# Two products of a fused model rewritten as sums of rounded parts, with buffers shared and three stages moved

## Chip, cores and metric

One core of a Trainium2 chip runs the whole kernel in one launch. The metric is device time in microseconds (us), lower is better; of several runs the median is compared.

## What is computed

Sixteen samples pass one after another through a chain of layers. Each sample is 384 rows of 256 numbers: 256 rows of image edges and 128 rows of embedded text.

```python
h = concat(edges(x), (U * s @ Vt)[x_txt])                 # 16 x 384 x 256
h = h + attention(layernorm(h))                           # 16 heads of 16, window of 128 rows
h = h + top_rows(layernorm(h))                            # 288 of 384 rows: gelu(row @ w_block)
h = h + state_space(layernorm(h))                         # circulant recurrence, by its DFT
xf = layernorm(h)
shared = gelu(xf @ sw1.T + sb1) @ sw2.T + sb2             # 256 -> 1024 -> 256, every row
logits = xf @ router_w.T + router_b                       # 8 experts, the best 2 of each row
h = h + shared + sum(weight_e * expert_e(xf))             # experts: 256 -> 1024 -> 256
```

The change touches `xf @ sw1.T` (the shared network's first product) and `xf @ router_w.T` (the router's).

## The kernel before

The five engines' programs are written out by hand, each in its own function, with semaphores between them; an engine runs its instructions strictly in that order. The samples form a software pipeline: `sequence(b)` runs, on each engine, the attention of sample b, together with the *head* of sample b+1 (edges, text, normalisation, queries, keys, values), the *chain* of sample b-1 (row selection, state space, router, first shared product) and the *late* part of sample b-2 (second shared product, slot rows for the experts). Sequences 0 and 1 and the last two are written out, since parts are missing there (sequence 0 has no chain); those between are a loop. After sequence 17 the experts' stage gathers rows by expert and runs in chunks to the end; the change touches its weights' loads only.

A sequence has 33 slots, s = 0 to 32. Slots 0 to 23 each start one *unit* of the attention (two heads for 128 query rows): PE makes scores, DVE their maximum (`mx`), ACT the exponentials (`prob`), PE turns them (two slots later), ACT evicts (`pT`), PE multiplies with the values. The rest is placed in numbered slots, and in its slot it stands in an engine's queue before or behind that slot's unit. These matter here:

- Slot 1, DVE: `own` (L1215) and the rank trials (L1221, L1224) of sample b-1, behind the eviction of `srow` on ACT (L844); the trials write their products into `rot` and `cum` and go on in slots 2 and 3. They stand before unit 1's maximum (L1150).
- Slots 2 to 8, PE: the six pieces of the second shared product (`down`, L1716), the text's turn in slot 3 and its product in slot 5 (L1564), which waits for DVE's `usT` (L1088, slot 4).
- Slot 21, DVE: `xn` of sample b+1 (L1063), then the third statistics of the chain (`chain_rows(b, 2)`, L1038). POOL then works out the deviations, DVE normalises `xc` in slot 26 (L1063), and POOL adds the shared network's bias (`shared_residual`, L666).
- Slots 24 to 27: ACT evicts xT (L789), PE multiplies the queries of b+1 (slot 26), turns xc and multiplies the keys (slot 27); ACT evicts the queries (q_hi, q_full) and then the turned xc as `xcT`; DVE splits the keys into k_hi and k_lo (L1118, L1122), then makes q_lo (L1129).
- Slots 28 to 32, PE: the logits (L1773), the values (L1600), the output product and the eight blocks f of the first shared product (`up`, L1703; six of them behind slot 32).

An f32 product appears on PE as two instructions for each pair of a weight tile and a moving tile. Where attention needs products of rounded parts already (scores, edges, experts), a float32 is held as `hi` (rounded to fp32r) and `lo` (the rest), and hi*hi + hi*lo + lo*hi is added up.

SP's queue (`stack(b + 1)`) copies the parts of the queries and keys into the stacked operands `qs` and `ks`, 36 transfers a sample in four pairs of head groups: 8 of q_hi, then for each pair 4 of k_hi, 1 of q_lo, 2 of k_lo. It starts when the queries are evicted (`q_ready`), behind the store of xc (`xn_rows`). Each pair has a semaphore `stacked[pair]`, and PE waits for it where the pair is first used:

```python
                    m, r = g % KB, g // KB
                    if i == 0 and m == 0:
                        pe.wait_ge(stacked[r].sem, stacked[r].at(b, stacked[r].per))
```

that is in slots 0, 2, 4 and 6. For sample 0 the keys are stacked by `stack_first_keys`, and DVE builds the powers of the recurrence's eigenvalues in slots 2 to 10 of sequence 0 (`powers`, which uses `rot`).

Of the kernel before, what the change touches and what calls it, by code (L numbers as in the profile page):

```python
# [57 lines left out]
LATER = (OUT + 2,)  # L58
# [21 lines left out]
def build(nc, t):  # L80
    with ExitStack() as ctx:
# [46 lines left out]
        rank_cols = sb("rank_cols", [P, T])  # L128
# [10 lines left out]
        rw = sb("rw", [P, KB, NE])  # L139
        rb_row = sb("rb_row", [P, NE])  # L140
        sw1 = sb("sw1", [P, KB, F])
# [45 lines left out]
        k_hi = room("k_hi", [P, KB, T], F32R)  # L187
        k_lo = room("k_lo", [P, KB, T], F32R)
# [16 lines left out]
        xc = room("xc", [P, NT, D])  # L205
        xcT = room("xcT", [P, KB, T])
# [4 lines left out]
        g = room("g", [P, NT, D])  # L211
        rot = room("rot", [P, 4, T])
        cum = room("cum", [P, 2, T])
        st = room("st", [P, 2, T])
# [4 lines left out]
        hb2 = room("hb2", [P, NT, D])  # L219
        hid = room("hid", [P, FB, T])  # L220
# [3 lines left out]
        dft, idft, b_w, c_wT = (mats[:, n] for n in range(4))  # L224
        place = place[:, 4 * KB * D:]
# [7 lines left out]
        with ExitStack() as space:  # L233
# [39 lines left out]
        late_loaded = dma_signal("late_weights_loaded", 0)  # L273
        set_up = signal("constants_ready", 0)
# [150 lines left out]
            (rb_row, t["rb"].partition_broadcast(P)), (sw1, t["sw1"]), (sw2, t["sw2"]), (sb1, t["sb1"]),  # L425
# [29 lines left out]
        def _(sp):  # L455
# [82 lines left out]
            load_image(1)  # L538
            load_halo(1)
# [46 lines left out]
        def _(pool):  # L586
# [174 lines left out]
        def _(act):  # L761
# [68 lines left out]
            def turned_rows(b, n):  # L830
# [8 lines left out]
                act.activation(xcT[:], ps[:, 6:8, 0:T], ACT.Copy).then_inc(xcT_ready.sem, 1)  # L839
# [29 lines left out]
            def sequence(b, att, late, chain, head, first_weights=False):  # L869
                for s in range(SLOTS):  # L870
                    if head and s in (CONV + 2, CONV + 4):
                        magnitude(b + 1, (s - CONV) // 2 - 1)
# [41 lines left out]
            sequence(0, True, False, False, True)  # L914
# [44 lines left out]
        def _(dve):  # L959
# [20 lines left out]
            def constants():  # L980
# [9 lines left out]
                for i in range(NT):  # L990
                    dve.tensor_scalar(before[:, i], rank_cols[:], rank_own[:, i:i + 1], None, ALU.is_lt)
                    dve.tensor_scalar(after[:, i], rank_cols[:], rank_own[:, i:i + 1], None, ALU.is_ge)
# [120 lines left out]
            def keys(b):  # L1113
# [5 lines left out]
                ins.then_inc(k_ready.sem, 1)  # L1119
                dve.wait_ge(k_ready.sem, k_ready.at(b, 1))  # L1120
# [88 lines left out]
            def chain(b, s, last):  # L1209
# [9 lines left out]
                if RANK <= s < RANK + NT:  # L1219
                    i = s - RANK  # L1220
                    dve.scalar_tensor_tensor(out=trial[2 * i], in0=srow[:], scalar=own[:, i:i + 1],  # L1221
                                             in1=before[:, i], op0=ALU.is_ge, op1=ALU.mult,
                                             accum_out=count[:, 0, i:i + 1])
                    ins = dve.scalar_tensor_tensor(out=trial[2 * i + 1], in0=srow[:], scalar=own[:, i:i + 1],  # L1224
                                                   in1=after[:, i], op0=ALU.is_gt, op1=ALU.mult,
# [49 lines left out]
                if s == OUT + 2:  # L1275
                    chain_rows(b, 2, last)
# [73 lines left out]
            def sequence(b, att, late, chained, head, ahead, first=False, first_weights=False):  # L1350
                att_step.steps = 0
                for s in range(SLOTS):
                    if first and s == 1:
                        eigenvalues()
                    if first and 2 <= s < 2 + (T - 1).bit_length():
                        powers(2 ** (s - 2))
                    if first_weights and s in (TURN1, STATE + 4):
                        split_first(s == STATE + 4)
                    if chained and s not in LATER:
# [9 lines left out]
                    if chained and s in LATER:  # L1369
# [5 lines left out]
                    if head and s == TEXT + 3:  # L1375
                        text_in(b + 1)
                    if first and s == TURN1 - 1:
# [6 lines left out]
                    if head and s == UP - 1:  # L1384
                        keys(b + 1)
# [41 lines left out]
            keys(0)  # L1427
# [4 lines left out]
            dve.wait_ge(late_loaded.sem, late_loaded.at(0, NLATE))  # L1432
            sequence(1, True, False, True, True, True)
# [90 lines left out]
        def _(pe):  # L1524
# [67 lines left out]
            def values(b):  # L1592

                pe.wait_ge(ctx_ready.sem, ctx_ready.at(b, 0))
                for i in range(NT):
# [5 lines left out]
                ins.then_inc(proj_done.sem, 1)  # L1601
# [96 lines left out]
            def up(b, f):  # L1698
# [70 lines left out]
            def logits(b):  # L1769
                    pe.wait_ge(xcT_ready.sem, xcT_ready.at(b, 3))  # L1770
                    for i in range(NT):
                        for k in range(KB):
                            ins = pe.matmul(ps[:, 7, i * NE:(i + 1) * NE], xcT[:, k, i * P:(i + 1) * P], rw[:, k],  # L1773
                                            start=(k == 0), stop=(k == KB - 1))
                    ins.then_inc(logit_done.sem, 1)

            def sequence(b, att, late, chained, head, first=False, last=False):
                for s in range(SLOTS):
# [8 lines left out]
                    if head and s == UP + 2:  # L1787
                        values(b + 1)
# [32 lines left out]
                    if chained and s == TURN2 + 1:  # L1821
# [29 lines left out]
            values(0)  # L1851
# [3 lines left out]
            pe.wait_ge(late_loaded.sem, late_loaded.at(0, NLATE))  # L1855
            sequence(1, True, False, True, True, first=True)
# [129 lines left out]
```

## Time and profile before

| | us |
|---|---|
| timed runs, median of 3 | 2091.02 (2086.0 to 2092.26) |
| profiled execution | 2075.45 |
| its span, first to last instruction | 2073.7 |
| PE busy in the span | 1952.0 (94%) |
| DVE, ACT, POOL busy | 1346.1, 1069.5, 766.6 |
| mean granted TensorE clock | 0.984 of 2.4 GHz |

The profile is one execution. A row of the timeline gives the start and the length of merged instructions; a PE row's length includes the drain of its last product, so products in a row are dated by their starts. `PEld` are PE's weight loads, `SPq` is SP's queue of transfers. In brackets stands the time that an engine sat idle and what ended it. Lines (L1703) are those of the kernel above.

### The profile page before, as it was taken

The numbers are of one execution on the slowest core, as the hardware profiler recorded it, in microseconds if no ns is written. First come the engines' busy times: TensorE is split into PE (matmuls) and PEld (weight loads), VectorE is DVE, ScalarE is ACT, GpSimd is POOL, SyncE is SP. The second block draws the span as 40 slices with busy tenths as digits, with TensorE's granted clock in tenths as the row PEclk, the third lists the DMA queues.
The fourth block names the chain that finished last, engine by engine and source line by source line (L and its number), as shares of the span: only waits on it lengthen the run. The fifth ranks groups of instructions, "written<-read, shape, count | busy, mean of one in ns | idle before, by whom it ended". The sixth has DMA issues, their size and how long they took to land.

```text
span 2073.7 us, 45068 instructions
## 1 busy us (share of the span) xinstructions
PE 1952.0 (94%) x13784; PEld 1572.3 (76%) x13864; DVE 1346.1 (65%) x3781; ACT 1069.5 (52%) x2509; POOL 766.6 (37%) x1269
## 2 busy tenths in 40 slices
PE   6789999999999999999999999888999999999997
PEld 5556766667666666676666766666999999999997
DVE  5767777677676676777767767655665555656553
ACT  1545545555455555554555545541555555555553
POOL 4012333324333243232332432305354455555554
PEclk9989999999999999999999999989999999999999
DMA  5222121120211202212112021110442332323222
GB/s 172 59 47 61 33 55 44 40 68 23 56 53 29 69 28 56 59 33 54 43 41 68 23 55 38 30 54 23 130 128 44 46 89 46 89 43 87 47 46 40
DMA packets 81091, 116.56 MB, mean 56 GB/s; under 512 B 20964, under 2 KB 61508, under 8 KB 78724
## 3 DMA queue, kind: packets, MB, share of 16 engines
q1 hardware_dynamic: 54372, 84.16, 14.6%
q0 software_dynamic: 23360, 27.91, 8.2%
q10 hardware_dynamic: 3312, 3.94, 0.7%
q8 instruction: 21, 0.34, 0.1%
q14 instruction: 26, 0.21, 0.0%
HBM read 51.58 MB, written 26.71 MB: 38 GB/s over the span
## 4 chain that ended last, share of the span: by engine, by line
PE 76%; DVE 11%; issue 8%; POOL 2%; ACT 2%; ACTq 1%; DVEq 0%; DMA 0%; POOLq 0%
PE ps L1888 14%; PE ps L1703 8%; PE ps L1716 5%; PE ps L1899 4%; PE ps L1900 4%; PE ps L1901 4%; PE ps L1633 4%; PE ps L1577 4%; PE ps L1652 3%; PE ps L1549 3%; PE ps L1625 3%; PE ps L1640 2%; PE ps L1694 2%; PE ps L1754 2%; PE ps L1689 2%
## 5 line engine op out<-in xcount | busy, mean ns | idle before, releaser
L819 ACT ACTIVATE prob<-ps,mx 128x256 f32<-128x256 f32 (+1 forms) x768 | 293.9, 441 | 206.9 <-DVE mx L1150 198.5
L1150 DVE TENSOR_REDUCE mx<-ps 128x2 f32<-128x512 f32 (+1 forms) x384 | 227.2, 596 | 205.5 <-PE ps L1625 195.7
L931 ACT ACTIVATE hid_hi<-ps,b 128x256 fp32r<-128x256 f32 x408 | 203.4, 498 | 275.9 <-PE ps L1888 275.9
L811 ACT ACTIVATE pT<-ps 128x512 f32<-128x512 f32 (+1 forms) x384 | 204.2, 532 | 134.8 <-PE ps L1633 132.4
L1479 DVE TENSOR_TENSOR hid_lo<-hid_full,hid_hi 128x256 fp32r<-128x256 f32 x408 | 171.3, 426 | 143.8 <-ACT hid_full L934 143.7
L732 POOL DMA_INDIRECT result<-yb,idx_o x102 | 176.6, 1732 | 165.0 <-DVE yb L1496 143.1
L1633 PE MATMUL ps<-ident,prob 128*128 128x128 f32 x1280 | 208.0, 277 | 26.8 <-ACT prob L819 26.8
L1899 PE MATMUL ps<-w_hi,hid_hi 128*128 128x256 f32 x816 | 230.0, 282 | 0.0
L1900 PE MATMUL ps<-w_lo,hid_hi 128*128 128x256 f32 x816 | 225.5, 276 | 0.0
L1901 PE MATMUL ps<-w_hi,hid_lo 128*128 128x256 f32 x816 | 225.3, 276 | 0.0
L1633 PEld LDWEIGHTS ps<-ident,prob 128*128 128x128 f32 x1280 | 160.5, 143 | 64.6 <-ACT prob L819 30.6
L934 ACT ACTIVATE hid_full<-ps,b 128x256 f32<-128x256 f32 x408 | 203.1, 498 | 0.0
L1625 PE MATMUL ps<-ks,qs 96*128 96x512 f32 (+1 forms) x384 | 199.9, 521 | 2.3 <-ACT prob L819 2.3
L676 POOL DMA_INDIRECT slot_rows<-pay,row_i x96 | 113.3, 1180 | 220.8 <-DVE tok L1339 196.3
L1716 PE MATMUL ps<-sw,hid 128*128 128x256 f32 x768 | 185.9, 387 | 2.3 <-ACT g L846 1.0
L1703 PE MATMUL ps<-xcT,sw 128*128 128x384 f32 x512 | 174.4, 494 | 0.2 <-ACT hid L855 0.2
L1888 PE MATMUL ps<-xg_hi,w_hi 128*128 128x256 f32 x816 | 165.1, 284 | 2.5 <-DVE xg_lo L1472 1.4
L1716 PEld LDWEIGHTS ps<-sw,hid 128*128 128x128 f32 x768 | 138.8, 190 | 34.2 <-issue 11.7
L1888 PE MATMUL ps<-xg_lo,w_hi 128*128 128x256 f32 x816 | 164.4, 283 | 0.0
L1888 PE MATMUL ps<-xg_hi,w_lo 128*128 128x256 f32 x816 | 164.4, 283 | 0.0
L1900 PEld LDWEIGHTS ps<-w_lo,hid_hi 128*128 128x128 f32 x816 | 153.4, 188 | 0.0
L1899 PEld LDWEIGHTS ps<-w_hi,hid_hi 128*128 128x128 f32 x816 | 153.3, 188 | 0.0
(283 smaller groups left out, 4109.3 us busy)
## 6 DMA issues: line engine op xcount, KB each, us to landing
w_raw<-in_w SPq DMA_DIRECT2D x16, 1024.0 KB, 6.4
xin<-in_x SPq DMA_DIRECT2D x32, 384.0 KB, 3.7
ks<-k_hi SPq DMA_DIRECT2D x256, 48.0 KB, 2.1
qs<-q_hi SPq DMA_DIRECT2D x120, 96.0 KB, 2.1
ks<-k_lo SPq DMA_DIRECT2D x128, 48.0 KB, 2.1
xn_rows<-xc SPq DMA_DIRECT2D x16, 384.0 KB, 2.5
result<-h SPq DMA_DIRECT2D x16, 384.0 KB, 2.6
qs<-q_lo SPq DMA_DIRECT2D x60, 96.0 KB, 2.1
```

The costliest lines, as they stand in the source:

```text
L811: act.activation(pT[:, u % TB, :, k0:2, :], ps[:, 2 + u % 2, :].rearrange("p (h k q) -> p h k q", h=2, k=2)[:, :, k0:2, :], ACT.Copy).then ...
L819: ins = act.activation(prob[:, s % PB, hh, w], ps[:, s % 2, hh * 2 * P + w.start:(hh + 1) * 2 * P], ACT.Exp, bias=mx[:, s % 2, hh:hh + 1])
L931: act.activation(hid_hi[:, f], ps[:, f % 4, 0:CHUNK], ACT.Gelu_apprx_tanh, bias=b1[half][:, f:f + 1])
L1150: dve.tensor_reduce(mx[:, s % 2], sc, AX_X, ALU.max, negate=True).then_inc(max_done.sem, 1)
L1625: pe.matmul(dst, qs[:, r, m, i * P:(i + 1) * P], ks[:, r, :, m, keys], start=False, stop=True).then_inc(scores_done.sem, 1)
L1633: ins = pe.transpose(ps[:, 2 + u % 2, (2 * hh + k) * P:(2 * hh + k + 1) * P], prob[:, u % PB, hh, k * P:(k + 1) * P], ident[:])
L1703: ins = pe.matmul(ps[:, 6 + f % 2, 0:T], sw1[:, k, f * P:(f + 1) * P], xcT[:, k], start=(k == 0), stop=(k == KB - 1))
L1716: ins = pe.matmul(tile_out(i), hid[:, f, i * P:(i + 1) * P], sw2[:, f], start=(f == 0), stop=(f == FB - 1))
L1888: ins = pe.matmul(ps[:, f % 4, 0:CHUNK], w[half][:, k, cols], x[:, k], start=(n == 0), stop=(n == len(terms) - 1))
L1899: pe.matmul(out, hid_hi[:, f, rows], w2_hi[half][:, f], start=(f == 0), stop=False)
L1900: pe.matmul(out, hid_hi[:, f, rows], w2_lo[half][:, f], start=False, stop=False)
L1901: ins = pe.matmul(out, hid_lo[:, f, rows], w2_hi[half][:, f], start=False, stop=(f == FB - 1))
```

## The change

The shared network's first product and the router's take xf and the weights as rounded parts: `sw1_hi`, `sw1_lo`, `rw_hi`, `rw_lo` are made once, `xcT_hi` comes from ACT's eviction (in the place of `xcT`), and `xcT_lo` from a new DVE instruction, `turned_rests`, between k_hi and k_lo in slot 27. Each product becomes three fp32r products. For room, k_hi and k_lo lie in `rot`, xcT_hi in xcT, xcT_lo in `st`, the raw sw1 in the place of the start's matrices, rank_cols in hb2; the two masks `before` and `after` become shifted views of one row each. Since the rank trials and the powers write `rot`, DVE first waits for the stacked semaphores of all four pairs: in slot 1, ahead of `own`, and in slot 1 of sequence 0, ahead of the powers. sw1 is loaded by SP after the start's matrices are read, rounded by ACT in slot 12 and subtracted by DVE in slot 15 of sequence 0; the router's parts are made ahead of sequence 1. The chain's third statistics move from slot 21 to slot 22, behind that slot's unit; POOL's shared residual waits for the normalised xc of that stage; the logits move from slot 28 to 29; two of the three values products move ahead of them, to slot 28; and SP loads the experts' biases later.

```diff
-LATER = (OUT + 2,)
+LAST_STATS = OUT + 3
...
-        before = sb("before", [P, NT, T], BF16)
-        after = sb("after", [P, NT, T], BF16)
+        before_w = sb("before_w", [P, T + 2 * P], BF16)
+        after_w = sb("after_w", [P, T + 2 * P], BF16)
...
-        k_hi = room("k_hi", [P, KB, T], F32R)
-        k_lo = room("k_lo", [P, KB, T], F32R)
...
+        with ExitStack() as shared:
+            k_hi = shared.enter_context(nc.sbuf_tensor("k_hi", [P, KB, T], F32R))
+            k_lo = shared.enter_context(nc.sbuf_tensor("k_lo", [P, KB, T], F32R))
         rot = room("rot", [P, 4, T])
...
+            sp.wait_ge(mats_read.sem, mats_read.at(0, 1))
+            sp.dma_start(sw1, t["sw1"]).then_inc(sw1_loaded.sem, 16)
...
+            sequence(NB, True, True, False, False)
+            sp.wait_ge(hb2_ready.sem, hb2_ready.at(NB, 0))
             for half in range(2):
                 load_biases(half, half)
-            sequence(NB, True, True, False, False)
...
             def shared_residual(b):
 
-                pool.wait_ge(h3_ready.sem, h3_ready.at(b, 1))
+                pool.wait_ge(xc_ready.sem, xc_ready.at(b, 3))
...
-                act.activation(xcT[:], ps[:, 6:8, 0:T], ACT.Copy).then_inc(xcT_ready.sem, 1)
+                act.activation((xcT if n < 2 else xcT_hi)[:], ps[:, 6:8, 0:T], ACT.Copy).then_inc(xcT_ready.sem, 1)
...
+            def round_shared():
+
+                act.wait_ge(sw1_loaded.sem, sw1_loaded.at(0, 16))
+                act.activation(sw1_hi[:], sw1, ACT.Copy).then_inc(sw1_rounded.sem, 1)
...
+            def split_shared():
+
+                dve.wait_ge(sw1_rounded.sem, sw1_rounded.at(0, 1))
+                dve.tensor_tensor(sw1_lo[:], sw1, sw1_hi[:], ALU.subtract)
...
+            def turned_rests(b):
+
+                dve.wait_ge(xcT_ready.sem, xcT_ready.at(b, 3))
+                dve.tensor_tensor(xcT_lo[:], ps[:, 6:8, 0:T], xcT_hi[:], ALU.subtract).then_inc(rest_ready.sem, 1)
+
-            def keys(b):
+            def keys(b, chained):
...
                 ins.then_inc(k_ready.sem, 1)
+                if chained:
+                    turned_rests(b - 2)
                 dve.wait_ge(k_ready.sem, k_ready.at(b, 1))
...
-                if s == OUT + 2:
+                if s == LAST_STATS:
                     chain_rows(b, 2, last)
...
                     if first and s == 1:
                         eigenvalues()
+                        for pair in range(PAIRS):
+                            dve.wait_ge(stacked[pair].sem, stacked[pair].at(b, stacked[pair].per))
...
+                    if chained and att and s == RANK:
+                        for pair in range(PAIRS):
+                            dve.wait_ge(stacked[pair].sem, stacked[pair].at(b, stacked[pair].per))
-                    if chained and s not in LATER:
+                    if chained and s != LAST_STATS:
                         chain(b - 1, s, not att)
...
-                for k in range(KB):
-                    ins = pe.matmul(ps[:, 6 + f % 2, 0:T], sw1[:, k, f * P:(f + 1) * P], xcT[:, k],
-                                    start=(k == 0), stop=(k == KB - 1))
+                terms = [(w, x, k) for w, x in ((sw1_hi, xcT_hi), (sw1_hi, xcT_lo), (sw1_lo, xcT_hi)) for k in range(KB)]
+                for n, (w, x, k) in enumerate(terms):
+                    ins = pe.matmul(ps[:, 6 + f % 2, 0:T], w[:, k, f * P:(f + 1) * P], x[:, k],
+                                    start=(n == 0), stop=(n == len(terms) - 1))
...
-                    pe.wait_ge(xcT_ready.sem, xcT_ready.at(b, 3))
+                    pe.wait_ge(rest_ready.sem, rest_ready.at(b, 1))
+                    terms = [(x, w, k) for x, w in ((xcT_hi, rw_hi), (xcT_hi, rw_lo), (xcT_lo, rw_hi)) for k in range(KB)]
                     for i in range(NT):
-                        for k in range(KB):
-                            ins = pe.matmul(ps[:, 7, i * NE:(i + 1) * NE], xcT[:, k, i * P:(i + 1) * P], rw[:, k],
-                                            start=(k == 0), stop=(k == KB - 1))
+                        for n, (x, w, k) in enumerate(terms):
+                            ins = pe.matmul(ps[:, 7, i * NE:(i + 1) * NE], x[:, k, i * P:(i + 1) * P], w[:, k],
+                                            start=(n == 0), stop=(n == len(terms) - 1))
...
                     if head and s == UP + 2:
-                        values(b + 1)
+                        values(b + 1, 2, NT)
...
-                    if chained and s == TURN2 + 1:
+                    if head and s == TURN2 + 1:
+                        values(b + 1, 0, 2)
+                    if chained and s == TURN2 + 2:
                         logits(b - 1)
```

## Rows read from the trace of the kernel before

**Rows 1.** Windows, one period: us; PE, PEld, DVE, ACT, POOL busy; clock; DMA; GB/s.

```profile
610.00:694.30 84.30, 81.19 (x530) 58.32 (x534) 59.54 (x175) 45.64 (x103) 27.85 (x61) 1.00 0.18 47
```

**Rows 2.** Timeline of SP's queue: start us, us, engine line op out<-in xcount.

```profile
609.97 5.05 SPq L445 DMA_DIRECT2D qs<-q_hi  x8
...
631.55 1.23 SPq L451 DMA_DIRECT2D ks<-k_lo  x2
```

**Rows 3.** DMA issues: out<-in queue op xcount, KB each, median us to landing.

```profile
ks<-k_lo SPq DMA_DIRECT2D x128, 48.0 KB, 2.1
```

**Rows 4.** Timeline, slots 1 to 5; in brackets idle time before and releaser.

```profile
631.19 0.29 DVE L1215 SCALAR_TENSOR_TENSOR rot<-srow,ident 128x128 f32<-128x128 f32 x1 [3.63 <-ACT srow L844]
...
636.50 0.42 DVE L1150 TENSOR_REDUCE mx<-ps 128x2 f32<-128x256 f32 x1 [1.64 <-PE ps L1625]
...
641.96 0.33 DVE L1088 TENSOR_SCALAR usT<-ps,s_col 64x128 f32<-64x128 f32 x1
...
642.35 0.70 PE L1564 MATMUL ps<-vt,usT 64*128 64x256 f32 x2
```

**Rows 5.** Timeline of PE, the router's product and the shared network's first.

```profile
611.06 1.40 PE L1773 MATMUL ps<-rw,xcT 128*128 128x8 f32 x12
...
617.68 9.19 PE L1703 MATMUL ps<-xcT,sw 128*128 128x384 f32 x28
```

**Rows 6.** Timeline of PE, fp32r products: gray rows (512 columns), experts (256 columns).

```profile
579.88 0.40 PE L1549 MATMUL ps<-gray_hi,band_lo 128*128 128x512 f32 x1
...
580.11 0.40 PE L1549 MATMUL ps<-gray_hi,band_hi 128*128 128x512 f32 x1
...
1599.99 0.28 PE L1899 MATMUL ps<-w_hi,hid_hi 128*128 128x256 f32 x1
1600.10 0.28 PE L1900 MATMUL ps<-w_lo,hid_hi 128*128 128x256 f32 x1
```

**Rows 7.** Timeline, slots 21 to 26 of the same period.

```profile
597.66 1.05 DVE L1063 TENSOR_SCALAR xn<-h,ln 128x256 f32<-128x256 f32 x3
...
598.64 1.07 DVE L1038 BATCH_NORM_STATS2 lnc<-hc 128x6 f32<-128x256 f32 x3
...
599.97 1.25 DVE L1150 TENSOR_REDUCE mx<-ps 128x2 f32<-128x512 f32 x2
...
601.56 0.66 PE L1633 MATMUL ps<-ident,prob 128*128 128x128 f32 x4 [1.77 <-ACT prob L819]
...
602.85 0.85 ACT L789 ACTIVATE xT<-ps 128x768 f32<-128x768 f32 x1
...
604.08 2.75 PE L1577 MATMUL ps<-xT,wq 128*128 128x384 f32 x8
...
604.75 2.19 POOL L666 TENSOR_TENSOR hb<-hc,sb_row 128x256 f32<-128x256 f32 x3
604.83 2.27 DVE L1063 TENSOR_SCALAR xc<-hc,lnc 128x256 f32<-128x256 f32 x3 [1.23 <-POOL lnc L632]
```

**Rows 8.** Timeline, sequence 0 (first two rows) and sequence 1.

```profile
54.23 0.42 DVE L1150 TENSOR_REDUCE mx<-ps 128x2 f32<-128x256 f32 x1
...
60.38 1.22 SPq L451 DMA_DIRECT2D ks<-k_lo  x2
...
129.26 0.29 DVE L1215 SCALAR_TENSOR_TENSOR rot<-srow,ident 128x128 f32<-128x128 f32 x1 [5.40 <-ACT srow L844]
...
133.33 1.23 SPq L451 DMA_DIRECT2D ks<-k_lo  x2
```

**Rows 9.** Timeline, the experts' first weights rounded and subtracted.

```profile
1391.62 1.90 ACT L866 ACTIVATE w_hi<-w_raw 128x2048 fp32r<-128x2048 f32 x1
...
1403.23 2.29 DVE L1348 TENSOR_TENSOR w_lo<-w_raw,w_hi 128x2048 fp32r<-128x2048 f32 x1
```

**Rows 10.** Windows in sequence 15, where the clock falls.

```profile
1343.60:1347.00 3.40, 1.07 (x19) 0.72 (x20) 2.83 (x5) 1.43 (x4) 0.92 (x1) 1.00 0.00 0
1347.00:1350.50 3.50, 3.50 (x12) 2.96 (x11) 0.69 (x1) 2.33 (x6) 0.00 (x0) 0.51 0.02 5
```

More of the change, by code:

```diff
@@ L127, in build @@
         wb = sb("wb", [P, KB, D])
-        rank_cols = sb("rank_cols", [P, T])
         rank_own = sb("rank_own", [P, NT])
-        before = sb("before", [P, NT, T], BF16)
-        after = sb("after", [P, NT, T], BF16)
+        before_w = sb("before_w", [P, T + 2 * P], BF16)
+        after_w = sb("after_w", [P, T + 2 * P], BF16)
+        before, after = ([w[:, (NT - 1 - i) * P:(NT - 1 - i) * P + T] for i in range(NT)] for w in (before_w, after_w))
         a_col = sb("a_col", [P, 1])
@@ L139, in build @@
         rw = sb("rw", [P, KB, NE])
+        rw_hi = sb("rw_hi", [P, KB, NE], F32R)
+        rw_lo = sb("rw_lo", [P, KB, NE], F32R)
         rb_row = sb("rb_row", [P, NE])
[L141 removed]
+        sw1_hi = sb("sw1_hi", [P, KB, F], F32R)
+        sw1_lo = sb("sw1_lo", [P, KB, F], F32R)
         sw2 = sb("sw2", [P, FB, D])
@@ L211, in build @@
         g = room("g", [P, NT, D])
+        with ExitStack() as shared:
+            k_hi = shared.enter_context(nc.sbuf_tensor("k_hi", [P, KB, T], F32R))
+            k_lo = shared.enter_context(nc.sbuf_tensor("k_lo", [P, KB, T], F32R))
         rot = room("rot", [P, 4, T])
         cum = room("cum", [P, 2, T])
+        with ExitStack() as shared:
+            xcT_lo = shared.enter_context(nc.sbuf_tensor("xcT_lo", [P, KB, T], F32R))
         st = room("st", [P, 2, T])
@@ L224, in build @@
         dft, idft, b_w, c_wT = (mats[:, n] for n in range(4))
+        sw1 = place[:, 0:KB * F].rearrange("p (k n) -> p k n", k=KB)
         place = place[:, 4 * KB * D:]
@@ L867, in round_first, with sequence @@
                 act.activation(w2_hi[0][:], w2_raw[:], ACT.Copy).then_inc(hi_ready.sem, 1)
-            def sequence(b, att, late, chain, head, first_weights=False):
+            def round_shared():
+                act.wait_ge(sw1_loaded.sem, sw1_loaded.at(0, 16))
+                act.activation(sw1_hi[:], sw1, ACT.Copy).then_inc(sw1_rounded.sem, 1)
+            def sequence(b, att, late, chain, head, first=False, first_weights=False):
                 for s in range(SLOTS):
+                    if first and s == TURN1:
+                        round_shared()
                     if head and s in (CONV + 2, CONV + 4):
@@ L913, in _ @@
             act.wait_ge(u_gathered.sem, u_gathered.at(0, 16 * (NB - 1)))
-            sequence(0, True, False, False, True)
+            sequence(0, True, False, False, True, first=True)
             act.wait_ge(late_loaded.sem, late_loaded.at(0, NLATE))
@@ L989, in constants @@
                 dve.tensor_copy(tok[:], rank_own[:])
-                for i in range(NT):
-                    dve.tensor_scalar(before[:, i], rank_cols[:], rank_own[:, i:i + 1], None, ALU.is_lt)
-                    dve.tensor_scalar(after[:, i], rank_cols[:], rank_own[:, i:i + 1], None, ALU.is_ge)
+                dve.memset(before_w[:, 0:2 * P], 1.0)
+                dve.memset(after_w[:, 0:2 * P], 0.0)
+                dve.tensor_scalar(before_w[:, 2 * P:], rank_cols, rank_own[:, 0:1], None, ALU.is_lt)
+                dve.tensor_scalar(after_w[:, 2 * P:], rank_cols, rank_own[:, 0:1], None, ALU.is_ge)
                 for k in range(KB):
@@ L1376, in sequence @@
                         text_in(b + 1)
+                    if first and s == CONV:
+                        split_shared()
                     if first and s == TURN1 - 1:
@@ L1384, in sequence @@
                     if head and s == UP - 1:
-                        keys(b + 1)
+                        keys(b + 1, chained)
+                    if chained and not head and s == UP - 1:
+                        turned_rests(b - 1)
                     if head and s == UP:
@@ L1590, in keys, with values @@
                 project(b, wk, 2)
-            def values(b):
+            def values(b, first, last):
                 pe.wait_ge(ctx_ready.sem, ctx_ready.at(b, 0))
-                for i in range(NT):
+                for i in range(first, last):
                     if i == 2:
@@ L1850, in _ @@
             keys(0)
-            values(0)
+            values(0, 0, NT)
             matrices()
```

24 lines of the change are left out of this document (18 added, 6 removed).

## Prediction

> **What bounds the kernel now.** I read the windows of one period of the sample loop first, then the queues' timeline, then the timeline of each engine around the places that the diff touches. The window is one whole period, from SP's first stacking transfer of one sample (610.0) to that of the next (694.3): PE is busy 81.19 of 84.30 us, at full clock, and no other engine above 60 [rows 1]. So the loop is bound by PE, and the reader is to see how little room that leaves: what takes PE's work away pays, what makes PE wait costs in full.
>
> A second thing goes on inside that period and costs nothing yet. SP issues the stacking transfers of the next sample in a row, 0.63 us each: eight of q_hi from 609.97, then k_hi, q_lo and k_lo, the last pair from 631.55 [rows 2]. The very last is issued at 632.17 and, with 2.1 us from issue to landing [rows 3], lands at 634.3, that is 24.3 us after the first issue. That train is as long as its 36 issues; nothing on PE makes it shorter. PE meets it pair by pair, the last pair only in slot 6, so it is hidden today. On DVE the `own` product of slot 1 starts at 631.19, when ACT has evicted `srow` [rows 4].
>
> **The wait for the stacks.** k_hi and k_lo now lie in `rot`, which slot 1 writes, so DVE waits in slot 1 until all four pairs have landed. Between 631.19 and 634.3 that is 3.1 us per sample. Behind it in DVE's queue stand `own`, the rank trials, the maxima of units 1 to 4, sumv, the slot rows, and usT; for usT waits PE's text product, and behind that stand two pieces of the down product and all later scores. DVE ran from 631.19 to the end of usT (641.96 + 0.33) in 11.1 us with one pause of 1.64, before the maximum of 636.50 [rows 4]. After the wait the pause is used up (ACT and PE are by then ready), so 9.5 us of work in a row follow on 634.3, and usT ends at 643.8 where it ended at 642.3: 1.5 us late. PE started the text 0.06 behind usT [rows 4], so PE and everything behind it move by 1.5. Bounds: nothing absorbed 3.1; that 0.4 more of later pauses is found, 1.1.
>
> **Three products for one.** A 384-column f32 product is two passes of instructions; 28 take 9.19 us, the last 0.49 of it a drain, so 0.322 each and 1.29 per block f [rows 5]. No fp32r product of 384 columns stands in the trace. At 256 columns they start 0.11 apart, at 512 columns 0.23 [rows 6]: these are the bounds, and 0.17 between them is my estimate. Six are then 1.04 per block, 0.25 less; over eight blocks PE gains 2.0 us (5.0 to a loss of 0.7). The router's product of 8 columns is 12 instructions in 1.40, 0.112 apart [rows 5]; 18 at that pace cost 0.67 more. Net 1.3 us less PE work per sample. But all of it stands after the queries' eviction that starts SP's train and before slot 1. The next sample's DVE waits for the train, 24.3 us after that start whatever PE does, so the 1.3 is spent waiting there: worth nothing in the loop. If the slowest pace held, PE would be late by up to 1.4, and the train still mostly covers it; I give 0.3 a sample for that end.
>
> The rest `xcT_lo` is one DVE subtraction of 768 elements between k_hi and k_lo, like the `q_lo` one about 1 us. It delays k_lo, q_lo and the last context by that. SP needs q_lo only eight q_hi and four k_hi after its start (7.6 us), and has it before; PE fills the time with the two values products put ahead of the logits. Cost nothing; without that cover, 1 us of PE.
>
> **Statistics and residual moved.** In slots 21 and 22 DVE does xn, then the chain's statistics at 598.64 (1.4 us with their aggregates), and only then the maximum of unit 22 at 599.97; PE stands 1.77 us until 601.56 for the exponential behind it [rows 7]. With the statistics one slot later that maximum goes first, 1.3 us earlier. The maximum of unit 23 then ends near 601.3, as before, but ACT has done unit 22's exponential by then; unit 23's follows at once, and xT, evicted behind it, moves from 602.85 to about 602.1. PE's transposes are no longer late either, so the queries start with xT's end, near 603.0 instead of 604.08 [rows 7]: 1.1 earlier, and that carries to the start of the train. The xc normalisation took 2.27 us beside POOL's shared residual of 604.75 where xn took 1.05 alone [rows 7]; with the residual behind xc it takes 1.05, which pays back the 0.7 by which its statistics are later, so it stays ready in time. I take 1.1 us gained per sample; bounds 0 and the whole pause, 1.8. The Trainium skill (SBUF — State Buffer, the section on what contends with what) says that DVE and GpSimd lock their shared port pair for a whole instruction. That agrees with 2.27 beside 1.05, and by it the residual now stands in the way of the gray products and perhaps k_hi; if that reached the path with 0.4 us a sample the sum would be 6 higher. The sum here leaves it out, because SP's q_hi transfers go first.
>
> **Start and end.** In sequence 0 the wait stands before the powers: the maximum of unit 1 ran at 54.23, the last k_lo is issued at 61.0 and lands at 63.1 [rows 3, 8]. 8.9 us, and DVE's row of powers behind it has no pause to give back. In sequence 1 no shared network stands between the queries and slot 1, so DVE is there early, at 129.26, and the last k_lo lands at 136.1 [rows 8]: 6.8 us, less a pause as in the loop, 5.2. Rounding the shared weights on ACT and subtracting on DVE, 2048 elements each, is 1.90 and 2.29 as for the experts' weights [rows 9]; half-hidden in sequence 0, I take 1.5 of 0 to 4.2. In the last sequence the rest and longer logits (+1.7) meet the shorter blocks (-2.0): nothing. The biases loaded later are needed only by the experts, after two more waits: nothing; they would cost one landing. The transfer of sw1 goes out ahead of sequence 0 and is used in slot 12: nothing.
>
> **Sum.** 8.9 + 1.5 + (5.2 - 1.1) + 14 sequences of (1.5 - 1.1) = 5.6: 20.1 us more. The profiled execution took 2075.45 (span 2073.7); the sum gives it 2095.6. The timed runs lie higher, median 2091.0, so the forecast is 2111: slower by 1.0%. Low end of its own: start 14, loop 14 x (1.1 - 1.8) = -10, in all about +3; high end: start 18, loop 14 x 1.5 + 4 = 25, +43, which needs all costs at once; its own range is 2097 to 2127.
>
> **Rivals.** (1) *PE's savings carry, faster.* PE is nearly always busy, for it; if the wait did not bind, each sample would gain 1.3 and 1.1, 14 x 2.4 = 34, less 14 at the start: 2071. It decides if the train ends 3.1 us sooner, 0.54 instead of 0.63 per issue; against it, the issue time is the same all along the train. Chance 0.10. The Trainium skill (FP8 and Floating Point Precision, TensorE Precision Notes) counts four passes for true FP32; three parts at one pass each would by that save a quarter of the 10.3 us, 2.6, and this rival would give 2062; no fp32r row here is at 384 columns.
> (2) *The wait is absorbed.* If DVE's lateness were lost in the time PE spends on down products in slots 3 to 6, the loop gains 1.1 a sample, 15, and that cancels the start: 2091. For it, four of the six down products stand in those slots and need nothing from DVE; against it, PE takes its work in order, and text waits on usT directly [rows 4]. Chance 0.13.
> (3) *The clock falls.* PE now stands some 2 us within slots 2 to 5. In a stretch where it was busy 1.07 of 3.40 the next stretch ran at 1.2 GHz (granted 0.51) for 3.5 us [rows 10]; one such stretch a sample costs half of it, 1.75 x 14 = 24 more: 2136. Against it: the pause of 1.77 us in slot 24 left the whole period at full clock [rows 1, 7]. The Trainium skill (TensorE: Matmul & The Clock Gate, Part 1) says that the throttled clock is the default and activity releases it, which is what these two stretches show. Chance 0.12.
>
> **Numbers.** The forecast has 0.65. Slower by over 0.3% (6 us, about what the runs' spread of 2086.0 to 2092.3 can tell from no change): forecast and (3), 0.77. Within: 0.13. Faster: 0.10. The range reaches down to (2) and up to the forecast's own high side, short of (3): 2089 to 2129.
>
> **What would show it.** In the profile after: DVE's `own` starting 24.3 us behind SP's first q_hi, released by a DMA, with about 6.8 us of idle time before it; usT 1.5 us later against SP's start; a period near 84.7; the pause before PE's transposes of slot 24 shrunk to about 0.5; xc at 1.05; unit 1 of sequence 0 at 63; fp32r products of 384 columns 0.17 apart. Wrong if the period is at or under 84.0, or if `own` is again released by ACT.

## The result, and the profile after

The changed kernel takes 2126.42 us (median of 4 runs, 2124.27 to 2128.83) against 2088.51 for the kernel before (2084.34 to 2092.26): ratio 1.0187, 95% interval 1.0166 to 1.0208. That is 38 us slower, where the forecast's terms made 20; 2126 lies in the range given, near its upper end.

One profile has to be set right first. In the profile of before on which the rows above rest, ScalarE had the first turned rows at 37.87 us. In the profile after, and in a second profile of before that I took (experiment 10), it had them 12 us later. The timeline of ScalarE, after and then before a second time:

```profile
50.17 0.81 ACT L806 ACTIVATE xT<-ps 128x768 f32<-128x768 f32 x1 [18.88 <-remote]
```

```profile
49.75 0.81 ACT L789 ACTIVATE xT<-ps 128x768 f32<-128x768 f32 x1 [18.85 <-remote]
```

Thirteen profiles of fourteen, all but the first, show this delay, whatever the edit, so it belongs to both kernels: the second profile of before has a span of 2085.6 where the first had 2073.7. The change is read against the second. SP's first stacking transfer of a sample marks the stages. After (SP's queue, and the experts' first product on PE):

```profile
135.19 1.21 SPq L459 DMA_DIRECT2D qs<-q_hi  x2
...
215.73 1.21 SPq L459 DMA_DIRECT2D qs<-q_hi  x2
...
302.34 1.21 SPq L459 DMA_DIRECT2D qs<-q_hi  x2
...
1325.49 0.57 SPq L459 DMA_DIRECT2D qs<-q_hi  x1
...
1499.98 0.63 PE L1930 MATMUL ps<-ident,xg 128*128 128x128 f32 x4 [1.19 <-DVE h L1353]
```

Before, second profile:

```profile
126.47 0.57 SPq L445 DMA_DIRECT2D qs<-q_hi  x1
...
202.14 1.21 SPq L445 DMA_DIRECT2D qs<-q_hi  x2
...
287.14 1.20 SPq L445 DMA_DIRECT2D qs<-q_hi  x2
...
1298.57 0.57 SPq L445 DMA_DIRECT2D qs<-q_hi  x1
...
1469.89 0.63 PE L1872 MATMUL ps<-ident,xg 128*128 128x128 f32 x4 [1.19 <-issue]
```

The differences of these rows, with the spans 2124.5 and 2085.6 as the end:

| stage | before | after | more | forecast |
|---|---|---|---|---|
| to the first transfer (sequence 0) | 126.5 | 135.2 | 8.7 | 10.4 |
| sequence 1 | 75.7 | 80.5 | 4.9 | 4.1 |
| the next period | 85.0 | 86.6 | 1.6 | 0.4 |
| twelve periods of the loop | 1011.4 | 1023.2 | 11.7 | 4.8 |
| last samples, to the experts | 171.3 | 174.5 | 3.2 | 0.4 |
| experts, to the end | 615.8 | 624.5 | 8.7 | 0 |

The forecast's 20.1 is its column; the measured column makes 38.8. Inside one period of after, SP's queue and then DVE and PE:

```profile
643.26 5.04 SPq L459 DMA_DIRECT2D qs<-q_hi  x8
...
664.82 1.23 SPq L465 DMA_DIRECT2D ks<-k_lo  x2
```

```profile
667.88 0.29 DVE L1257 SCALAR_TENSOR_TENSOR rot<-srow,ident 128x128 f32<-128x128 f32 x1 [7.97 <-DMA ks<-k_lo]
...
677.02 0.33 DVE L1113 TENSOR_SCALAR usT<-ps,s_col 64x128 f32<-64x128 f32 x1
```

```profile
670.86 0.39 PE L1677 MATMUL ps<-mask_bf,ident_bf 128*128 128x256 bf16 x1 [1.84 <-ACT prob L836]
...
671.89 3.09 PE L1770 MATMUL ps<-sw,hid 128*128 128x256 f32 x8
```

`own` comes 24.6 us behind the train's start and is released by a DMA, where ACT released it at 21.2 [rows 2, 4]; usT is 33.8 behind that start instead of 32.0. PE then stands 1.84 us, and the down product behind it runs at little more than half its pace: eight instructions in 3.09 us, where the same eight take 1.89 in the sample before. The windows show the clock at its lower level, 1.2 GHz, right there (columns as in [rows 1]):

```profile
643.30:728.90 85.60, 82.08 (x552) 62.57 (x556) 59.72 (x177) 45.80 (x103) 28.89 (x62) 0.98 0.18 46
...
667.50:670.90 3.40, 1.56 (x11) 0.93 (x9) 2.98 (x14) 1.54 (x7) 0.00 (x0) 1.00 0.02 5
670.90:674.30 3.40, 3.40 (x11) 2.93 (x12) 3.20 (x20) 1.31 (x5) 0.00 (x0) 0.50 0.00 1
```

That happens in five of the twelve periods of the table, every second one from 472.6 on; those take 85.6, the others 85.0 (the first 85.2, the last 84.8). The pause is as long in the others. Here is PE in the sample before, whose clock stays full:

```profile
585.81 0.28 PE L1677 MATMUL ps<-mask_bf,ident_bf 128*128 128x256 bf16 x1 [1.83 <-ACT prob L836]
...
586.38 1.89 PE L1770 MATMUL ps<-sw,hid 128*128 128x256 f32 x8
...
592.38 0.70 PE L1616 MATMUL ps<-vt,usT 64*128 64x256 f32 x2 [0.67 <-DVE usT L1113]
```

So PE waits twice behind the train: for the exponential of unit 1, and 0.67 us for usT. In a sample with the low clock it is late by more than 0.67 at the text product and doesn't wait there; that is why its period is longer by 0.58 only, and not by the 1.2 us that the eight instructions lose.

The end of the period, answering to [rows 7], on DVE, PE and POOL:

```profile
717.61 1.05 DVE L1088 TENSOR_SCALAR xn<-h,ln 128x256 f32<-128x256 f32 x3
718.58 0.68 DVE L1192 TENSOR_REDUCE mx<-ps 128x2 f32<-128x512 f32 x1
719.18 1.07 DVE L1063 BATCH_NORM_STATS2 lnc<-hc 128x6 f32<-128x256 f32 x3
...
725.32 1.06 DVE L1088 TENSOR_SCALAR xc<-hc,lnc 128x256 f32<-128x256 f32 x3 [2.63 <-POOL lnc L649]
```

```profile
720.19 0.66 PE L1686 MATMUL ps<-ident,prob 128*128 128x128 f32 x4 [0.46 <-ACT prob L836]
```

```profile
726.46 3.11 POOL L683 TENSOR_TENSOR hb<-hc,sb_row 128x256 f32<-128x256 f32 x3 [1.17 <-DVE xc L1088]
```

The maximum goes ahead of the statistics, the pause before the turns is 0.46 instead of 1.77, xc takes 1.06 instead of 2.27. And the products, on PE, six to a block of the shared network:

```profile
652.72 0.51 PE L1757 MATMUL ps<-xcT_hi,sw_hi 128*128 128x384 f32 x2
653.07 0.52 PE L1757 MATMUL ps<-xcT_lo,sw_hi 128*128 128x384 f32 x2
653.43 0.51 PE L1757 MATMUL ps<-xcT_hi,sw_lo 128*128 128x384 f32 x2
653.77 0.34 PE L1757 MATMUL ps<-xcT_hi,sw_hi 128*128 128x384 f32 x1
```

They start 0.175 apart, 1.05 a block (653.77 - 652.72) where four instructions took 1.29 [rows 5].

### The profile page after: what moved, and what is told of

The parts are those of the page before. It is cut to its first block, busy times and chain, and to the rows that moved or that the text cites. A ratio compares the mean times of both kernels' runs of the same rounds, so it can differ in the third digit from the quotient of the medians.

```text
span 2124.5 us, 45853 instructions
## 1 busy us (share of the span) xinstructions
PE 1964.2 (92%) x14136; PEld 1639.9 (77%) x14216; DVE 1351.6 (64%) x3798; ACT 1072.7 (50%) x2510; POOL 779.4 (37%) x1269
## 4 chain that ended last, share of the span: by engine, by line
PE 60%; SPq 14%; issue 10%; DVE 7%; POOL 3%; ACT 2%; DMA 2%; ACTq 1%; DVEq 0%; POOLq 0%
PE ps L1946 14%; SPq L465 9%; PE ps L1770 5%; SPq L459 5%; PE ps L1958 5%; PE ps L1957 5%; PE ps L1959 5%; PE ps L1686 4%; PE ps L1705 3%; PE ps L1601 3%; PE ps L1678 3%; PE ps L1629 2%; PE ps L1808 2%; PE ps L1677 2%; DMA ks<-k_lo 1%
## 5 line engine op out<-in xcount | busy, mean ns | idle before, releaser
L1531 DVE TENSOR_TENSOR hid_lo<-hid_full,hid_hi 128x256 fp32r<-128x256 f32 x408 | 171.3, 425 | 143.9 <-ACT hid_full L958 140.0
L1770 PE MATMUL ps<-sw,hid 128*128 128x256 f32 x768 | 194.4, 400 | 2.3 <-ACT g L863 1.0
L1770 PEld LDWEIGHTS ps<-sw,hid 128*128 128x128 f32 x768 | 145.6, 199 | 36.3 <-issue 12.7
L1677 PE MATMUL ps<-mask_bf,ident_bf 128*128 128x512 bf16 (+1 forms) x305 | 106.2, 348 | 61.2 <-ACT prob L836 51.4
```

The costliest lines, as they stand in the source:

```text
L1770: ins = pe.matmul(tile_out(i), hid[:, f, i * P:(i + 1) * P], sw2[:, f], start=(f == 0), stop=(f == FB - 1))
```

## The experiments

**1. The wait by itself.** The kernel before, with the keys' parts laid on the rotations' buffer and both waits; products and moves stay.

```diff
-        k_hi = room("k_hi", [P, KB, T], F32R)
-        k_lo = room("k_lo", [P, KB, T], F32R)
+        room("k_room", [P, 2 * KB * T])
...
+        with ExitStack() as shared:
+            k_hi = shared.enter_context(nc.sbuf_tensor("k_hi", [P, KB, T], F32R))
+            k_lo = shared.enter_context(nc.sbuf_tensor("k_lo", [P, KB, T], F32R))
         rot = room("rot", [P, 4, T])
...
+                    if chained and att and s == RANK:
+                        for pair in range(PAIRS):
+                            dve.wait_ge(stacked[pair].sem, stacked[pair].at(b, stacked[pair].per))
```

> The kernel before, in which only the keys' parts lie on the rotations' buffer and VectorE has the two new waits (sequence 0 and slot 1); products, statistics and residual are those of before. Theory (the wait is the cost, at my terms): +8.9 in sequence 0, +4 to +5 in sequence 1, +1.5 to +2 for each of 14 samples, in all +34 to +42: 2123 to 2130 us, with the diagonal (own) 0.3 us behind the last landing of a k_lo part. Rival (the slot-1 wait is absorbed in the loop, and the added time is of the products and the moves): only the start, +9 to +14: 2098 to 2103 us, period 84.3.

Measured: 2124.98 us, ratio 1.018 (1.0161 to 1.0198). DVE, then PE, then one period:

```profile
671.29 0.29 DVE L1217 SCALAR_TENSOR_TENSOR rot<-srow,ident 128x128 f32<-128x128 f32 x1 [7.04 <-DMA ks<-k_lo]
```

```profile
674.27 0.28 PE L1631 MATMUL ps<-mask_bf,ident_bf 128*128 128x256 bf16 x1 [0.89 <-ACT prob L821]
...
674.84 1.89 PE L1723 MATMUL ps<-sw,hid 128*128 128x256 f32 x8
```

```profile
646.70:732.70 86.00, 81.42 (x530) 58.25 (x534) 59.48 (x175) 45.80 (x103) 27.92 (x61) 1.00 0.19 46
```

The waits alone cost 37 us. The period is 86.01 on the mean of twelve, 1.72 more than before. PE's pause is only 0.89 here, and no period of the twelve has a low stretch of the clock (the same eight instructions take 1.89).

**2. The waits taken away.** In after, slot 1's `own` and trials and sequence 0's powers write to `cum`, which is free then. Sequence 0's wait goes; the other moves to slot 14, where `rot` is then first written.

```diff
-            trial = [rot[:, 0], rot[:, 1], rot[:, 2], rot[:, 3], cum[:, 0], cum[:, 1]]
+            trial = [cum[:, n % 2] for n in range(2 * NT)]
...
-                    if chained and att and s == RANK:
+                    if chained and att and s == STATE:
...
-                dve.tensor_scalar(rot[:, 0, 0:m], turn[:, 0, 0:m], re, None, ALU.mult)
+                dve.tensor_scalar(cum[:, 0, 0:m], turn[:, 0, 0:m], re, None, ALU.mult)
```

> The changed kernel with the ranks' trials and sequence 0's powers written to the sums' buffer (cum), so that VectorE waits for the keys' stacking only in slot 14; buffers, products and moves are those of after. Theory (the waits are the whole cost, and the cheaper products save PE time that nothing else was able to use): without the waits 8.9 + 4 + 1.8 + 12 x 1.0 = 27 go, 2099 us; if the products' 1.3 us of each sample then shorten the period too, 2081 us and a period of 83. Rival (the split of the turned rows and the later logits themselves hold up the chain): stays above 2110, period above 84.6.

Measured: 2079.24 us, ratio 0.9947 (0.9932 to 0.9961), 47 less than after. On DVE `own` is released by ACT again, and one period is:

```profile
638.33 0.29 DVE L1257 SCALAR_TENSOR_TENSOR cum<-srow,ident 128x128 f32<-128x128 f32 x1 [3.61 <-ACT srow L861]
```

```profile
618.10:700.40 82.30, 80.34 (x552) 61.21 (x556) 60.17 (x177) 45.58 (x103) 28.80 (x62) 1.00 0.19 48
451.90:535.80 83.90, 81.97 (x552) 62.63 (x556) 60.26 (x177) 45.60 (x103) 28.81 (x62) 0.98 0.19 47
```

The theory's second case holds: without the waits the cheaper products do shorten the period. Three periods of the twelve have 83.9, with a low stretch of the clock.

**3. The moves put back.**

```diff
-LAST_STATS = OUT + 3
+LAST_STATS = OUT + 2
...
-                pool.wait_ge(xc_ready.sem, xc_ready.at(b, 3))
+                pool.wait_ge(h3_ready.sem, h3_ready.at(b, 1))
```

> The changed kernel with the third statistics back a slot and GpSimd's residual back behind the block's sum (h3), as before the change. Theory (the move is worth the 1.1 us of a sample that I counted): 14 x 1.1 more than after, 2142 us, xc behind residual at 2.2 us again and a pause ahead of the slot-24 transposes of 1.5 or more. Rival (the pause there is filled by the wait's delay anyway): 2126 us, within 3.

Measured: 2145.6 us, 19 more than after. PE and DVE at the old order:

```profile
727.12 0.66 PE L1686 MATMUL ps<-ident,prob 128*128 128x128 f32 x4 [1.78 <-ACT prob L836]
```

```profile
730.40 2.26 DVE L1088 TENSOR_SCALAR xc<-hc,lnc 128x256 f32<-128x256 f32 x3 [1.24 <-POOL lnc L649]
```

The mean period is 86.34, 1.08 above after: the moves are worth what I counted.

**4 and 7. Where the experts' buffers lie.** Their places depend on all that is allocated ahead of them; the change puts them 4736 bytes higher. Experiment 4 pads after by another 3456, experiment 7 pads before by the 4736 (the same edit with 656).

```diff
             ones1 = room("ones1", [P, NE])
+            b1 = [room(f"b1_{j}", [P, FB]) for j in range(2)]
+            b2_row = [room(f"b2_row{j}", [P, D]) for j in range(2)]
+            room("pad", [P, 336])
...
-            b1 = [room(f"b1_{j}", [P, FB]) for j in range(2)]
-            b2_row = [room(f"b2_row{j}", [P, D]) for j in range(2)]
+            room("hole", [P, 528])
```

> The changed kernel with the experts' buffers 3456 bytes higher (8192 above their places in before instead of 4736), the biases in front of them; nothing else. Theory (the experts' second product runs at 117.6 ns instead of 113.3 because of where its operands lie): back to 113.3 ns, 8.7 us less than after, 2118 us. Rival (another chip or another execution runs these products so): 2126 us, and the pace of these products is that of the kernel after, or another one that does not go with the place.

> The kernel before with the experts' buffers 4736 bytes higher, where the change puts them, the biases in front of them; nothing else. Theory (the pace of the experts' second product goes with the place of its operands): 117.6 ns instead of 113.3, the experts' part 624 us instead of 616, 2096 us. Rival (it goes with the program's code or with the execution): 113.3 ns, 2088 us. Its profile also shows whether the 12 to 14 us in which ScalarE waits for the first turned rows, 50 us instead of 38 in the five profiles after the first, belong to before as well: then its span is 2088 or more, not 2075.

Measured: experiment 4, 2121.56 us, ratio 1.0145 (1.0125 to 1.0165), 5 less than after where the theory had 8.7: the second product runs at 113.8 and 117.8 ns by turns from chunk to chunk, and the experts' stage takes 621.0. Experiment 7, 2096.69 us, ratio 1.003 (1.0018 to 1.0042), 117.8 ns throughout, stage 625.4, and a span of 2095.4 with the late first rows. So the place matters, and 6 us of the change's time are had by moving buffers alone.

**5. The moves by themselves**, the reverse of experiment 3 on the kernel before.

```diff
-LATER = (OUT + 2,)
+LATER = (OUT + 3,)
...
-                pool.wait_ge(h3_ready.sem, h3_ready.at(b, 1))
+                pool.wait_ge(xc_ready.sem, xc_ready.at(b, 3))
...
-                if s == OUT + 2:
+                if s == OUT + 3:
                     chain_rows(b, 2, last)
```

> The kernel before with the third statistics a slot later and GpSimd's residual behind the normalised rows (xc, 3), and nothing else of the change. Theory (the moves are worth the 1.1 us a sample that putting them back cost): period 83.2 instead of 84.3, 15 us less than before: 2073 us. Rival (the moves help only where the slot-1 wait has made the end of the sample late): period 84.3, 2088 us, within 3.

Measured: 2079.8 us, ratio 0.9948 (0.9933 to 0.9964); period 83.45, 0.84 less than before, the pause ahead of the turns 0.45. By itself the move pays a little less than the 1.1.

**6 and 11. The clock.** Products of the identity (14, then 7) put into the pause behind the wait, into columns that nothing reads.

```diff
+                    if chained and att and s == BLOCK + 1:
+                        for n in range(14):
+                            pe.matmul(ps[:, 7, T:T + P], ident[:], ident[:], start=True, stop=True)
                     if att:
                         unit(b, s)
```

> The changed kernel with 14 products of the identity by itself (128 columns, into unused columns) on TensorE in the pause behind the slot-1 wait. Theory (half of what the loop costs beyond my forecast is the clock, which falls in every second sample behind the pause of 1.84 us): no row at 1.2 GHz in the loop, period 85.0 in every sample instead of 85.03 and 85.61 by turns, some 4 us less than after: 2122 us. Rival (the alternation comes from elsewhere): period and time of after, 2126 us, or worse by what the products delay.

> The changed kernel with 7 products of the identity by itself in the pause behind the slot-1 wait. With 14 they were 28 instructions and ran 3.29 us, longer than the pause of 1.84, so that TensorE came 1.2 us late; 7 take some 1.6 us and fit. Theory (the clock's fall behind the pause costs the alternation of 85.03 and 85.61, 0.3 us a sample on average): no low rows in the loop, period 85.0 or a little under in every sample, 3 to 5 us less than after in the sum of the loop, 2122 us. Rival (the fall costs nothing that the pause in slot 24 doesn't give back): 85.3 on average, 2126 us, within 3.

Measured: 2126.15 and 2123.52 us; both intervals (1.0157 to 1.0192, 1.0146 to 1.0187) overlap that of after, so the time alone decides nothing. In experiment 6 the 14 products ran 3.29 us as 28 instructions, longer than the pause, and made PE late:

```profile
671.34 3.29 PE L1856 MATMUL ps<-ident 128*128 128x128 f32 x28
```

In both the alternation is gone: ten and nine of the twelve periods lie between 85.0 and 85.2, and no stretch behind slot 1 is low. The theory's "no low rows" does not hold, though: one period of experiment 6 (86.6) and the first six of experiment 11 have a low stretch at another place, behind the router's products. Four of those six are 85.0 to 85.1 all the same: PE comes late to slot 1, and the 0.67 us of waiting for usT are gone. The mean of experiment 11 is 85.12 against 85.26 after. So the fall behind the pause costs 0.58 in a period that has it; over after's twelve that is 85.26 - 85.03 = 0.23.

**8. Sequence 0 alone**: only the powers go to `cum`, slot 1 keeps its wait.

> The changed kernel with sequence 0's powers alone written to the sums' buffer, so that the wait in sequence 0 is gone and those of slot 1 stay. Theory (the term of 8.9 us is right, and the rest of the sum stands apart from it): 8 to 9 us less than after, 2118 us, first product of sequence 0 released by its own stacking, loop period of after (85.3). Rival (the stall only moves to sequence 1, whose wait takes it over): 2125 us, within 3.

Measured: 2119.37 us, 7 less than after. In after DVE stood 8.31 us in sequence 0:

```profile
77.59 0.42 DVE L1192 TENSOR_REDUCE mx<-ps 128x2 f32<-128x256 f32 x1 [8.31 <-DMA ks<-k_lo]
```

Here the first transfer goes out at 127.2 instead of 135.2, and the loop is that of after (85.29). The term stands apart.

**9. Both remedies**: experiment 2 with the pad of experiment 4.

> The trials and powers apart (2079 us) with the experts' buffers 3456 bytes higher and the biases in front, a try for a version faster than both. If the places set the pace of the experts' second product: half or more of 8.7 us less, 2070 to 2075 us, and 113 ns in at least half of the chunks. If the pace belongs to the execution: 2079 us within 4, pace 113, 117 or a mix.

Measured: 2072.04 us, ratio 0.9911 (0.9897 to 0.9926): faster than both kernels, and the best of this study. The second product runs at 113 ns in all chunks (113.4 on the mean); experts, first after and then experiment 9:

```profile
1701.07 0.28 PE L1958 MATMUL ps<-w_lo,hid_hi 128*128 128x256 f32 x1
...
1701.77 0.28 PE L1958 MATMUL ps<-w_lo,hid_hi 128*128 128x256 f32 x1
```

```profile
1699.73 0.28 PE L1958 MATMUL ps<-w_hi,hid_lo 128*128 128x256 f32 x1
...
1700.41 0.28 PE L1958 MATMUL ps<-w_hi,hid_lo 128*128 128x256 f32 x1
```

Between the two rows lie six products: 0.70 and 0.68 us.

**10. Before, profiled again.**

> The kernel before, profiled a second time. If the late first rows (ScalarE released at 50 us instead of 38) belong to its usual execution: a span near 2088. If the pace of the experts' second product goes with places: 113.3 ns throughout again; if with the execution: 117.6 or a mix.

Measured: 2087.44 us, first rows at 49.75, pace 113 ns throughout.

**12. The products by themselves**: experiment 9 with the edit of experiment 3.

> The version of 2072 us (trials and powers apart, experts' buffers moved) with the third statistics and the residual back at their old places, so that of the change only the products and the shared buffer are left. Theory (without the slot-1 wait the cheaper products carry, and the moves are worth 0.85 us a sample as in the run with the moves alone): period 83.3 instead of 82.4, 2084 us. Rival (the moves bring nothing once TensorE has less to do): period 82.4, 2072 us, within 3; other rival (the products bring nothing without the moves): period 84.3, 2095 us.

Measured: 2092.85 us, ratio 1.0017 (1.0003 to 1.003). By the time it looks as if the products bring nothing. The windows of two neighbouring samples, and of the place where they part, in the first and then in the second:

```profile
625.20:708.40 83.20, 80.08 (x557) 61.24 (x556) 60.53 (x176) 45.67 (x103) 27.93 (x61) 1.00 0.19 48
708.40:793.10 84.70, 81.61 (x557) 62.68 (x556) 60.60 (x176) 45.66 (x103) 27.96 (x61) 0.98 0.18 47
...
626.90:630.30 3.40, 3.37 (x25) 2.89 (x24) 3.37 (x7) 0.00 (x0) 0.00 (x0) 1.00 0.64 153
630.30:633.70 3.40, 3.40 (x19) 2.98 (x19) 3.03 (x21) 2.03 (x3) 0.00 (x0) 1.00 0.49 105
...
710.30:713.70 3.40, 3.37 (x25) 2.88 (x24) 3.37 (x7) 0.00 (x0) 0.00 (x0) 1.00 0.68 162
713.70:717.10 3.40, 3.40 (x12) 3.02 (x11) 3.03 (x22) 1.43 (x2) 0.00 (x0) 0.50 0.41 91
```

Four of the twelve periods are 83.2, as the theory said; the other eight are 84.7, each with the clock at 1.2 GHz right behind the router's products. The saving of 1.1 is there, and the clock takes 1.5 back in two samples of three. What decides in which is open: in both samples the router's products come at the same place, with PE busy 3.37 of 3.40 us. More is lost outside the loop: the experts' part, with its pace by turns, takes 621.2 where before a second time took 615.8.

## Why the forecast held in direction and missed in size

**The wait** (1.5 a sample): right in kind, a little small. `own` behind the train, released by a DMA, usT late by 1.8, the text product waiting for it: as said. Alone it is 1.72 (experiment 1). The idle time of DVE is 7.97 where it is 7.04 with the wait alone (6.8 forecast), because PE, with its cheaper products, delivers the scores for the maximum before it 0.9 earlier: SP's train sets slot 1, and the saving is spent there. The forecast let PE stand at the text product alone; most of its standing comes earlier, at the exponential of unit 1.

**The products** (nothing in the loop): right for the reason given. Spacing 0.175 against my 0.17. The Trainium skill (FP8 and Floating Point Precision, TensorE Precision Notes) counts four passes for true FP32, by which three parts, taken at one pass each, would save a quarter; an f32 product of two instructions takes 2 x 0.322 = 0.644, which is 3.7 of the 0.175 and not 4, and the block saves a fifth (1.29 to 1.05). The measurement decides. Taking the waits away frees the saving (experiment 2). In periods at full clock: before 84.3, moves alone 83.45, products alone 83.2, both 82.3; 0.85 and 1.1 add up to 2.0. What I missed is that a saving spent in waiting is not free: it makes PE's pause 1.84 instead of 0.89, and the clock falls behind the longer one, behind the shorter never. It does so in five periods of twelve; in the other seven the same pause leaves the clock full, and no run shows what decides. That is rival (3), in five periods of twelve at 0.58 instead of in each at 1.75.

**The moves** (-1.1): right, 1.08 by experiment 3, 0.84 by experiment 5; the pause of 0.46 and xc at 1.06 too. The residual now runs 3.11 beside the gray products instead of 2.19. With that the rule of the Trainium skill (SBUF — State Buffer, Who interferes with whom) agrees; but xc put back beside the residual costs 2.26 again, and the moves gain, so the 6 us that I set beside the rule did not come.

**Start**: 8.7 against 10.4. The stall is 8.31 against 8.9; with the wait gone sequence 0 keeps 0.7 more (127.2 in experiment 8 against 126.5), which leaves that for the rounding of sw1 where I took 1.5. Sequence 1 is 4.9 against 4.1: by itself the wait costs 6.1 there (experiment 1) instead of 5.2, and the moves give 1.2 (experiment 5).

**The step that failed is the sum.** It has no term for where the unchanged buffers come to lie, which is 8.7 of the 18.7 missing between the profiles, and 6.0 by the timed runs of experiment 7. Of the rest 6.9 are the loop: 0.98 a sample instead of 0.4, from a wait of 1.72 instead of 1.5, the clock's 0.23, and 0.13 left over, less than the two values of the moves (1.08 and 0.84) lie apart.

4.0 come from the period ahead of the loop and the last samples, where I gave 0.4 each. In the period ahead of the loop the wait costs 2.0 by itself (87.0 in experiment 1 against 85.0) and the moves give 0.6 (84.4 in experiment 5), which makes 1.4 of its 1.6. In the last samples the wait costs only 0.6 by itself, although PE stands 3.0 us behind it in after, and the clock falls; experiments 2 and 9, which have no wait in slot 1, are there 2.5 and 2.3 above before. A part is the rest `xcT_lo`. PE stands ahead of the router's products until DVE has made it, after and then before a second time:

```profile
1410.96 0.59 PE L1828 MATMUL ps<-rw_hi,xcT_hi 128*128 128x8 f32 x2 [1.04 <-DVE xcT_lo L1151]
...
1474.46 0.39 PE L1828 MATMUL ps<-rw_hi,xcT_hi 128*128 128x8 f32 x2 [1.89 <-DVE xcT_lo L1151]
```

```profile
1381.29 1.50 PE L1773 MATMUL ps<-rw,xcT 128*128 128x8 f32 x12 [0.46 <-ACT xcT L839]
...
1443.50 1.50 PE L1773 MATMUL ps<-rw,xcT 128*128 128x8 f32 x12 [0.90 <-ACT xcT L839]
```

That is 1.6 us, which the prediction had set against the shorter blocks. The two profiles of before lie 2.4 apart in this stage (173.8 and 171.3), so the remainder can't be told from chance. Start and sequence 1 together are 0.9 under.

That 2126 still lies in the range says little for the sum. The range's high side was built from a dearer start and loop, and the buffers' place, which brings 6.0 of the 38, had no term in it. And the sum was added to 2091.0, the median of three runs, where with the fourth it is 2088.5: by luck that took 2.5 off the miss.

**Rivals.** (1) Savings that carry: shown false for this kernel and true once slot 1 no longer waits. (2) Absorption: false, experiment 1 pays 1.72 a period for the wait. (3): above.

What stays open: why the place of the operands sets a pace. At 4736 bytes above before, seven profiles of seven run the second product at 117.8 ns, but for one to three chunks at the start of some (after itself from its fourth chunk on); at the old place and at 8192 above, four of seven have 113 throughout and three alternate by chunk. So something in the execution has a part as well, and no run here separates the two. The timed runs hint at it too, without showing it, as they leave no profile: of experiment 12's twelve, two lie at 2086.4 and 2086.8 and ten at 2092.1 to 2097.6, some 5 us apart, as the two kinds of experts' part are (615.5 in experiment 9, 621.2 in the profile of experiment 12).

## What to carry to other kernels

A buffer that shares room with the source of a transfer train inherits that train's end as a release: before sharing, look for the first writer of the shared room, and move scratch results out of it, as here the trials to `cum`. A saving on the bounding engine that ends in a fixed wait is lost, and here the pause that it lengthened cost some more by the clock. After any change of allocation compare the pace of unchanged stages as well.

## What the runs showed of the hardware that I had not expected

- The same products of 256 columns run at 113.4 or 117.8 ns with nothing changed but the places of the experts' buffers (experiments 10 and 7): 6 us of 2090.
- In experiment 12 the clock fell to 1.2 GHz behind a stretch in which PE was busy 3.37 of 3.40 us, with the router's 18 products of 8 columns and their weight loads in it. In the sample before, a stretch with the same products and the same busy share was followed by full clock. So a high busy share did not keep it up each time, and a pause of 1.83 (after) brought it down only at times, one of 0.89 (experiment 1) never.
- PE's six turns of the first rows start between 37.0 and 37.6 in after, but ScalarE is released at 50.1, with no work of either engine between. Thirteen profiles of fourteen have it; its cause is open.
